# A fused transformer kernel: attention on 32-wide array tiles, split scales moved ahead, and a new order of loads, banks and ranks

## The chip, the cores and the metric

The kernel runs on one core of a Trainium2 chip. A core has a matrix engine (TensorE, PE in the rows; its loads of the stationary operand are listed apart as PEld), a vector engine (VectorE, DVE), an engine for activation functions (ScalarE, ACT), a general one (GpSimd, POOL), and SyncE (SP), which here only issues transfers. Each engine works through its own instructions in their order and waits at counting semaphores for the others. The metric is the device time of one launch, in microseconds; less is better.

## The reference

Four layers run one after the other on x of 2 batches x 1024 rows x 512 columns, each as `x = layernorm(x + layer(x))`:

```python
# 1: linear attention, 16 heads of 32
q, k, v = elu(x @ Wq.T) + 1, elu(x @ Wk.T) + 1, x @ Wv.T          # by head
kv = einsum('bhtd,bhte->bhde', k, v)
z  = 1 / (einsum('bhtd,bhd->bht', q, k.sum(axis=2)) + 1e-6)
y  = einsum('bhtd,bhde,bht->bhte', q, kv, z) @ Wo.T
# 2: feed-forward with packed fp4 weights, 1408 wide, a scale for each group of 128
w  = lut[nibble(packed)] * repeat(scales_f16, 128)
y  = rms_norm((silu(x @ w_gate.T) * (x @ w_up.T)) @ w_down.T)
# 3: gated linear attention (one head of 32 keys), gate, norm
q, k = softmax(x @ Wq.T), sigmoid(x @ Wk.T);  g = log_sigmoid(-k)
o  = gla_chunk(q, k, x, g)
go = o @ Wog.T + x @ Wig.T
y  = (rms_norm(o) * norm_w * silu(go)) @ Wo.T
# 4: a router picks the 512 best of each batch's 1024 rows; those pass an expert of 2048
s  = x @ router_w + router_b;  top, idx = top_k(s, 512)
y  = scatter_add(sigmoid(top) * (gelu(x[idx] @ w1 + b1) @ w2 + b2))
```

## The kernel before

All of it is written out by hand in two functions of engine blocks: for each engine a list of helper calls in the order in which they run, with semaphores between. Nothing else sets the order.

**Products.** A product of two float32 operands is made of three matmuls on rounded halves, `three_products` (L38): high x high (L41), high x low (L42), low x high (L43). ScalarE writes a high half, VectorE (or GpSimd) the low one by a subtraction. "A product" below means one such matmul of 512 columns.

**linear_attention (L150).** A batch b has 8 tiles of 128 rows, n or t. `tile_kv` projects a tile to keys and values (8 x 3 products), ScalarE takes exp and copies the values into v1 (with a column of ones, for the sum of the keys), `keys` on VectorE makes the feature map, and `add_kv` adds the tile's k^T v1 to an accumulator in PSUM. It takes a group g of four heads at once, so its 128x129 result also holds products of unlike heads. After the eighth tile `sums` masks these away (`kvz`). `query(b, h, m)` projects a half batch h of 512 rows to queries of the group m; `numerators(b, t)` multiplies a tile's queries by kvz (four matmuls of 128x132, one a group, the last four columns being the denominators); `attend` on VectorE divides; `transpose_att` turns the tile, `att_high` and `att_low` split it, and `project_out` multiplies by Wo; `finish` and `normalise` on VectorE end the layer norm. PSUM has eight banks of 512 columns. Beside all this VectorE and ScalarE unpack the fp4 weights of layer 2 (`nibbles`, `values`), and ScalarE widens the gate scales. A barrier of all engines ends the function.

**feed_forward_to_end (L843).** Layer 2 works on 4 blocks b of 512 rows and 11 tiles j of the hidden width, in units of half a tile (gate, then up). PE makes 4 groups a unit (L2127, L2128: two matmuls each), ScalarE scales the first group into an accumulator (L1257), VectorE adds the other three (`groups`, L1543, each with the group's scale), GpSimd multiplies gate by up and makes the low half, and PE runs the down product some tiles later. The down weights are made in block 0: for each tile j the row of fp16 scales is loaded to all partitions, VectorE splits it into a high and a low part (`down_scales(j)`, L1529 mask and L1532 subtraction, 128x512), and GpSimd multiplies the unpacked values by both (`down_weights`). Three of the eleven packed down tiles are unpacked here too, with one shift and one mask (`nibbles`, L1518 and L1520).

Layer 3 takes the same blocks as n = 0..3 (LAST = 3). In each, a loop over t makes scores and state of 128 rows (`update` L2213, `scores` L2220, `outputs`), then four gating steps (`silu`, `p_high`, `gated`, `p_low`) and the output projection with `y_bank(n, t)`, and `residual`, `variance`, `normalise` and `router` of the block before follow on VectorE while the next runs. Batch 0 is complete after block 1, so its ranks are counted while blocks 2 and 3 run: `rank(0, t)` compares a tile's scores with all (L1729), GpSimd `scatter`s row numbers and weights by rank, and `gather` fetches the 512 chosen rows, whose transposes (L2310) open layer 4. Meanwhile the expert's weights are loaded in chunks and split (`upper_half`, `lower_half`, L1704). Layer 4 runs `up(b, j)` and `down(b, j)` for batch 0, then 1, and `last_downs` ends it, tile by tile; `finish_selected(t)` (from L1787) makes the last rows.

## Time and profile before

| | |
|---|---|
| median of three runs | 1006.41 us (1006.1, 1006.41 and 1541.61) |
| profiled execution | 1005.34 us, span 1003.6 us |
| mean granted clock of PE | 0.986 of full speed |
| busy over the span | PE 928.8 us (93%), DVE 668.7 (67%), ACT 402.1 (40%), POOL 303.9 (30%) |
| moved | 52.64 MB, 52 GB/s |

The span runs from the first to the last instruction that the profiler shows; the time of the execution is 1.74 us longer. A busy share is an average over layers with different limits, and an engine may be busy and yet not be what the end waits for. The run of 1541.61 us stands far from the two others, and the median doesn't depend on it.

### The profile page before, as it was taken

To read this page: it belongs to the slowest core of one execution; us is meant where nothing else is said; L and a number is where in the kernel's file an instruction comes from. 1 tells how busy PE (TensorE), PEld (TensorE's weight loads), DVE (VectorE), ACT (ScalarE), POOL (GpSimd) and SP (SyncE) were. 2 spreads that over 40 slices of the span, in tenths; PEclk is the share of its full clock that TensorE was granted. 3 is DMA by queue.
4 is the path that set the end of the run, shared out by engine and by line. 5 is a ranking of instruction groups with operands and counts; after the bars stand their busy time and mean duration, and the time that the engine had idled before them with its cause. 6 is when DMAs were issued, how large, how long until landed. Compare 5 with 4: busy or idle time off the path is not lost.

```text
span 1003.6 us, 12375 instructions
## 1 busy us (share of the span) xinstructions
PE 928.8 (93%) x4182; PEld 728.5 (73%) x4182; DVE 668.7 (67%) x1325; ACT 402.1 (40%) x673; POOL 303.9 (30%) x270
## 2 busy tenths in 40 slices
PE   7998999898899999999998998999989989999993
PEld 5786788776576786776776666686857768878883
DVE  4666752666998778778856876866676777455413
ACT  4543022222334444454546367554454244323220
POOL 1000100001676543443333412232215322633333
PEclk9999999998999999999999999999999999999997
DMA  8433101201000000000010020010200444231411
GB/s 281 143 99 108 43 22 42 74 11 54 17 16 17 1 1 1 1 1 0 1 42 1 0 95 1 1 43 1 85 1 23 126 136 123 68 126 42 148 63 42
DMA packets 41792, 52.64 MB, mean 52 GB/s; under 512 B 5889, under 2 KB 23681, under 8 KB 41729
## 3 DMA queue, kind: packets, MB, share of 16 engines
q1 hardware_dynamic: 39904, 47.63, 14.7%
q0 software_dynamic: 1824, 4.22, 1.3%
q8 instruction: 34, 0.56, 0.2%
q14 instruction: 30, 0.24, 0.1%
HBM read 41.33 MB, written 10.50 MB: 52 GB/s over the span
## 4 chain that ended last, share of the span: by engine, by line
PE 42%; DVE 19%; issue 8%; ACT 4%; POOL 2%; DVEq 0%; ACTq 0%; POOLq 0%
PE ps_gla L41 10%; PE ps_gla L43 10%; PE ps_gla L42 10%; DVE acc L1543 9%; PE ps_gla L2127 4%; PE ps_gla L2128 4%; ACT acc L1257 1%; DVE junk L1729 1%; PE ps_gla L2227 1%; DVE router_junk L1697 1%; PE ps_gla L2157 1%; ACT fjunk L791 1%; PE ps_gla L2213 1%; DVE gsg L1655 1%; DVE scale_lo L1532 1%
## 5 line engine op out<-in xcount | busy, mean ns | idle before, releaser
L1543 DVE SCALAR_TENSOR_TENSOR acc<-ps_gla,gu_scale,acc 128x512 f32<-128x512 f32 x264 | 196.3, 749 | 64.9 <-ACT acc L1257 42.6
L2127 PE MATMUL ps_gla<-xt_hi,gu_val 128*128 128x512 f32 x352 | 147.3, 418 | 18.0 <-DVE acc L1543 7.0
L2128 PE MATMUL ps_gla<-xt_lo,gu_val 128*128 128x512 f32 x352 | 139.8, 397 | 0.0
L2127 PEld LDWEIGHTS ps_gla<-xt_hi,gu_val 128*128 128x128 f32 x352 | 67.2, 191 | 59.1 <-DVE acc L1543 40.7
L1257 ACT ACTIVATE acc<-ps_gla,gu_scale 128x512 f32<-128x512 f32 x88 | 60.5, 688 | 114.4 <-PE ps_gla L2128 114.4
L2034 POOL TENSOR_TENSOR fsg<-fsg,acc 128x512 f32<-128x512 f32 x44 | 62.1, 1412 | 129.3 <-DVE acc L1543 129.3
L616 POOL TENSOR_TENSOR a_rstd<-a_var,minus_half 128x1 f32<-128x1 f32 x16 | 10.8, 676 | 226.2 <-DVE a_var L508 226.2
L2128 PEld LDWEIGHTS ps_gla<-xt_lo,gu_val 128*128 128x128 f32 x352 | 67.5, 192 | 11.0
L2039 POOL TENSOR_TENSOR fh_lo<-fsg,fh_hi 128x512 fp32r<-128x512 f32 x44 | 56.8, 1291 | 51.8 <-ACT fh_hi L1269 51.8
L41 PE MATMUL ps_gla<-dn_hi,fh_hi 128*128 128x512 f32 x176 | 69.5, 395 | 0.0
L42 PE MATMUL ps_gla<-dn_hi,fh_lo 128*128 128x512 f32 x176 | 69.0, 392 | 0.0
L43 PE MATMUL ps_gla<-dn_lo,fh_hi 128*128 128x512 f32 x176 | 68.7, 390 | 0.0
L2091 POOL TENSOR_TENSOR mh_lo<-mh,mh_hi 128x512 fp32r<-128x512 f32 x32 | 42.3, 1322 | 82.3 <-ACT mh_hi L1502 82.2
L1497 ACT ACTIVATE mh<-ps_gla,b_sb 128x512 f32<-128x512 f32 x32 | 22.0, 687 | 96.7 <-PE ps_gla L43 94.0
L41 PE MATMUL ps_attn<-a_w_hi,xt_hi 128*128 128x512 f32 x128 | 52.5, 410 | 7.3 <-DVE a_w_lo L527 6.7
L41 PE MATMUL ps_gla<-mxt_hi,mw_hi 128*128 128x512 f32 x128 | 51.0, 398 | 3.9 <-DVE mw_lo L1704 2.9
L42 PE MATMUL ps_attn<-a_w_hi,xt_lo 128*128 128x512 f32 x128 | 51.1, 399 | 0.0
L43 PE MATMUL ps_attn<-a_w_lo,xt_hi 128*128 128x512 f32 x128 | 51.1, 399 | 0.0
L42 PE MATMUL ps_gla<-mxt_hi,mw_lo 128*128 128x512 f32 x128 | 50.5, 395 | 0.0
L43 PE MATMUL ps_gla<-mxt_lo,mw_hi 128*128 128x512 f32 x128 | 50.5, 394 | 0.0
L41 PE MATMUL ps_gla<-mw_hi,mh_hi 128*128 128x512 f32 x128 | 49.9, 390 | 0.0
L42 PE MATMUL ps_gla<-mw_hi,mh_lo 128*128 128x512 f32 x128 | 49.8, 389 | 0.0
(274 smaller groups left out, 2202.1 us busy)
## 6 DMA issues: line engine op xcount, KB each, us to landing
mw_raw<-in_w SPq DMA_DIRECT2D x16, 512.0 KB, 3.6
a_nib<-in_gate_up_packed SPq DMA_DIRECT2D x88, 64.0 KB, 2.2
x<-x SPq DMA_DIRECT2D x16, 256.0 KB, 3.6
mw_raw<-x SPq DMA_DIRECT2D x8, 512.0 KB, 4.4
out<-mw_raw SPq DMA_DIRECT2D x8, 512.0 KB, 3.0
xt_raw<-in_xT SPq DMA_DIRECT2D x3, 1024.0 KB, 5.1
x<-in_x SPq DMA_DIRECT2D x3, 1024.0 KB, 5.8
a_nib<-in_down_packed SPq DMA_DIRECT2D x8, 256.0 KB, 3.1
```

The source lines that it names most:

```text
L41: pe.matmul(out, lh, rh, start=first, stop=False)
L42: pe.matmul(out, ll, rh, start=False, stop=False)
L43: return pe.matmul(out, lh, rl, start=False, stop=last)
L616: pool.tensor_tensor(rstd[i % 2][:, :], var[i % 2][:, :], const.minus_half[:, 0:1], ALU.pow).then_inc(s_rstd, 1)
L1257: act.activation(acc[part][u // 2 % 2][:, :], ps[:, FG, :], ACT.Copy, scale=gu_scale[:, part * IT + j, 0:1]).then_inc(s_g0, 1)
L1497: act.activation(h[j % 2][:, :], ps[:, H + j % 4, :], ACT.Gelu_apprx_tanh, bias=b1_sb[:, j:j + 1]).then_inc(m_g, 1)
L1543: dve.scalar_tensor_tensor(out=a[:, :], in0=ps[:, FG + c, :], scalar=gu_scale[:, part * IT + j, c:c + 1], in1=a[:, :], op0=ALU.mult, op1=A ...
L2034: pool.tensor_tensor(f_sg[k % 2][:, :], f_sg[k % 2][:, :], acc[1][k % 2][:, :], ALU.mult).then_inc(s_h, 1)
L2039: pool.tensor_tensor(f_lo[k % HS][:, :], f_sg[k % 2][:, :], f_hi[k % HS][:, :].bitcast(F32), ALU.subtract).then_inc(s_hl, 1)
L2091: pool.tensor_tensor(h_lo[j % HS][:, :], h[j % 2][:, :], h_hi[j % HS][:, :].bitcast(F32), ALU.subtract).then_inc(m_hl, 1)
L2127: pe.matmul(ps[:, FG + c, :], gu_val[:, o, c, :], xt_hi[b % 2][:, c, :], start=True, stop=False)
L2128: pe.matmul(ps[:, FG + c, :], gu_val[:, o, c, :], xt_lo[b % 2][:, c, :], start=False, stop=True).then_inc(s_gu, 1)
```

## The change

1. **Array tiles.** `add_kv` makes one matmul for each of the 16 heads instead of four for groups: 32 columns of keys as the stationary operand, 33 columns of v1, into a 32-partition strip of one bank. `kvz` is then a plain copy. `numerators(b, t)` does tiles t and t + 1 in one call, 16 matmuls each that contract over the 32 rows of one head; the four heads of a group go to four banks. `attend` does three VectorE operations instead of five.
2. **Order in the attention.** The queries of the second half are projected earlier (0 before the first numerators, 1 before the first transposes, 2 after them), with places of their own (`q_next`) and a table of banks. Transposes, projections and VectorE's list follow in a new order.
3. **First loads.** SyncE loads Wk, then the second x tile, then Wv; PE starts with seven matmuls of ones, then the keys of tiles 0 and 1, then their values. ScalarE widens the gate scales at tile 5, not 0.
4. **Down scales.** They are split in the attention, on 11 partitions at once, stored to a scratch tensor in DRAM, and loaded from there to all partitions as two halves, into four buffers. `down_scales` goes; the nibble steps of block 0 are spread over units 3 to 8.
5. **Banks and ranks.** Below LAST `y_bank` alternates between two banks; in block 2 two ranks remain (of three), in block 3 the others stand elsewhere, as do `variance`, `normalise(2)`, `router(2)`, `lower_half(3)` and `pair_weights(0)`.
6. **End.** `last_downs` is called by piece; the final semaphores are cleared without a barrier behind.

```diff
@@ add_kv, numerators, attend @@
                 for g in range(KC):
-                    ins = pe.matmul(ps[:, KV0 + g // 2, (g % 2) * (P + 1):(g % 2 + 1) * (P + 1)], k[n % 2][:, g * P:(g + 1) * P],
-                                    v1[n % 2][:, g, :], start=(n == 0 and g % 2 == 0), stop=(n == NT - 1), skip_group_check=True)
+                    for j in range(HG):
+                        h = HG * g + j
+                        ins = pe.matmul(ps[j * DH:(j + 1) * DH, KV, g * (DH + 1):(g + 1) * (DH + 1)], k[n % 2][:, h * DH:(h + 1) * DH],
+                                        v1[n % 2][:, h, :], start=(n == 0 and g == 0), stop=(n == NT - 1), skip_group_check=True)
...
-                for g in range(KC):
-                    ins = pe.matmul(ps[:, PROJ + 2 * (t % 2) + g // 2, (g % 2) * (P + HG):(g % 2 + 1) * (P + HG)],
-                                    q[:, g, col:col + P], kvz[:, g, :], start=True, stop=True)
-                ins.then_inc(s_num, 1)
+                for u in (t, t + 1):
+                    for g in range(KC):
+                        for j in range(HG):
+                            d = slice(j * DH, (j + 1) * DH)
+                            ins = pe.matmul(ps[:, PROJ + j, num_col(u, g)], query_out(b, h, g)[d, (u % TB) * P:(u % TB + 1) * P], kvz[d, g, :],
+                                            start=True, stop=True)
+                    ins.then_inc(s_num, 1)
...
+                if i == 0:
+                    dve.wait_ge(s_dss, 32)
+                done(dve.tensor_scalar(z[:, :].rearrange("p (j g) -> p j g", j=HG), num[:, :, :, DH], 1e-6, None, ALU.add))
                 done(dve.reciprocal(zi[t % 2][:, :], z[:, :]))
...
@@ PE's list in the attention @@
+            warm_up(WARM)
             for b in range(NB):
-                tile_kv(b, 0)
-                if b:
-                    transpose_att(0, NT - 1)
+                if b == 0:
+                    for w in (WK, WV):
+                        tile_kv(b, 0, (w,))
+                        tile_kv(b, 1, (w,))
+                    add_kv(b, 0)
+                else:
+                    tile_kv(b, 0)
...
                     query(b, 0, m)
+                query(b, 1, 0)
                 numerators(b, 0)
-                numerators(b, 1)
+                query(b, 1, 1)
                 transpose_att(b, 0)
+                transpose_att(b, 1)
+                query(b, 1, 2)
                 numerators(b, 2)
...
@@ down scales: split in the attention, loaded as parts @@
+                        elif n == 6:
+                            dve.wait_ge(s_ds, 16)
+                            dve.tensor_scalar(dn_scale_hi[:, :].bitcast(U16), dn_scale16[:, :].bitcast(U16), 0xFFFE, None,
+                                              ALU.bitwise_and).then_inc(s_dsp, 1)
+                            dve.wait_ge(s_dsp, 1)
+                            dve.tensor_tensor(dn_scale_lo[:, :], dn_scale16[:, :], dn_scale_hi[:, :], ALU.subtract).then_inc(s_dsp, 1)
...
-                sp.dma_start(scale[j % 2][:, :], dn_scales[j:j + 1, :].to_broadcast([P, C])).then_inc(s_scl[j % 2], 16)
+                i = j % SCALES
+                if j >= SCALES:
+                    sp.wait_ge(s_dl, j - SCALES + 1)
+                sp.dma_start(scale_hi[i][:, :], dn_parts[0, j:j + 1, :].to_broadcast([P, C])).then_inc(s_scl[i], 16)
+                sp.dma_start(scale_lo[i][:, :], dn_parts[1, j:j + 1, :].to_broadcast([P, C])).then_inc(s_scl[i], 16)
...
@@ VectorE, gated attention @@
-                    if n == LAST:
-                        rank(0, 3 + t)
                     if n:
                         residual(n - 1, t)
                     if t:
                         o_low(n, t - 1)
-                if 0 < n < LAST:
+                    if n == LAST:
+                        rank(0, 2 + t)
+                if n:
                     variance(n - 1)
                 o_low(n, TB - 1)
                 mean_square(n)
+                if n == LAST:
+                    rank(0, 6)
+                    rank(0, 7)
...
                 if n == 2:
-                    for t in range(3):
+                    for t in range(2):
                         rank(0, t)
...
             variance(LAST)
+            lower_half(3)
             normalise(LAST)
             router(LAST)
...
@@ y_bank, and PE's end @@
-            return (Y, F)[t % 2] if n == LAST else Y
+            return (Y, F if n == LAST else G + 1)[t % 2]
...
-            for j in range(2, FT):
+            for j in range(2, FT - 1):
                 up(1, j)
                 down(1, j - 2)
-            last_downs(FT - 2)
+            up(1, FT - 1)
+            for t in range(2):
+                last_downs(t, range(FT - 3, FT - 1))
+            for t in range(2):
+                last_downs(t, range(FT - 1, FT))
+            for t in range(2, TB):
+                last_downs(t, range(FT - 3, FT))
```

How the instructions stand before, on PE, at the first numerators of batch 0 (a_q the queries, a_att a divided tile, a_at its transposed halves):

```order
L41 MATMUL ps_attn<-xt_hi_53,a_w_hi_63 128x512
L42 MATMUL ps_attn<-xt_hi_53,a_w_lo_67 128x512
L43 MATMUL ps_attn<-xt_lo_55,a_w_hi_63 128x512
L675 MATMUL ps_attn<-a_kvz,a_q 128x132 x8
L686 MATMUL ps_attn<-ident,a_att_74 128x128 x4
L675 MATMUL ps_attn<-a_kvz,a_q 128x132 x4
L686 MATMUL ps_attn<-ident,a_att_75 128x128 x4
L41 MATMUL ps_attn<-a_w_hi_64,a_at_hi_76 128x512
```

And now, at the same numerators:

```order
L41 MATMUL ps_attn<-xt_hi_54,a_w_hi_63 128x512
L42 MATMUL ps_attn<-xt_hi_54,a_w_lo_67 128x512
L43 MATMUL ps_attn<-xt_lo_56,a_w_hi_63 128x512
L740 MATMUL ps_attn<-a_kvz,a_q 128x33 x32
L41 MATMUL ps_attn<-xt_hi_54,a_w_hi_63 128x512
L42 MATMUL ps_attn<-xt_hi_54,a_w_lo_67 128x512
```

and where the first transposes follow:

```order
L41 MATMUL ps_attn<-xt_hi_54,a_w_hi_63 128x512
L42 MATMUL ps_attn<-xt_hi_54,a_w_lo_67 128x512
L43 MATMUL ps_attn<-xt_lo_56,a_w_hi_63 128x512
L753 MATMUL ps_attn<-ident,a_att_74 128x128 x4
L753 MATMUL ps_attn<-ident,a_att_75 128x128 x4
L41 MATMUL ps_attn<-xt_hi_54,a_w_hi_63 128x512
```

What moved: 32 tile matmuls stand at once for two tiles, with products of query(0,1,0) ahead of them; another projection of queries stands between them and the transposes, which now come in a pair.

VectorE in block 0 of the feed-forward, before (acc the accumulators of groups, scale_hi and scale_lo the split row, nib a packed tile):

```order
L1543 SCALAR_TENSOR_TENSOR acc_0_2649<-ps_gla,gu_scale,acc_0_2649 128x512 x3
L1529 TENSOR_SCALAR scale_hi_2664<-scale_2662 128x512
L1532 TENSOR_TENSOR scale_lo_2666<-scale_2662,scale_hi_2664 128x512
L1543 SCALAR_TENSOR_TENSOR acc_1_2648<-ps_gla,gu_scale,acc_1_2648 128x512 x3
L1543 SCALAR_TENSOR_TENSOR acc_1_2650<-ps_gla,gu_scale,acc_1_2650 128x512 x3
L1529 TENSOR_SCALAR scale_hi_2665<-scale_2663 128x512
L1532 TENSOR_TENSOR scale_lo_2667<-scale_2663,scale_hi_2665 128x512
L1518 TENSOR_SCALAR nib_2659<-nib_2659,shift 128x512
L1520 TENSOR_SCALAR nib_2659<-nib_2659 128x512
L1543 SCALAR_TENSOR_TENSOR acc_0_2647<-ps_gla,gu_scale,acc_0_2647 128x512 x3
```

and now:

```order
L1606 SCALAR_TENSOR_TENSOR acc_0_2997<-ps_gla,gu_scale,acc_0_2997 128x512 x3
L1606 SCALAR_TENSOR_TENSOR acc_0_2999<-ps_gla,gu_scale,acc_0_2999 128x512 x3
L1606 SCALAR_TENSOR_TENSOR acc_1_2998<-ps_gla,gu_scale,acc_1_2998 128x512 x3
L1606 SCALAR_TENSOR_TENSOR acc_1_3000<-ps_gla,gu_scale,acc_1_3000 128x512 x3
L1585 TENSOR_SCALAR nib_3009<-nib_3009,shift 128x512
L1606 SCALAR_TENSOR_TENSOR acc_0_2997<-ps_gla,gu_scale,acc_0_2997 128x512 x3
L1589 TENSOR_SCALAR nib_3009<-nib_3009 128x512
L1606 SCALAR_TENSOR_TENSOR acc_0_2999<-ps_gla,gu_scale,acc_0_2999 128x512 x3
L1585 TENSOR_SCALAR nib_3010<-nib_3010,shift 128x512
L1606 SCALAR_TENSOR_TENSOR acc_1_2998<-ps_gla,gu_scale,acc_1_2998 128x512 x3
```

What moved: the masks and subtractions of the scales are gone, and a nibble step stands alone between three accumulations and the next three.

VectorE in block 3 of the gated attention, after its last tile of outputs, before (junk and counts are a rank's, gsg the gate, x the rows):

```order
L1643 TENSOR_TENSOR o_lo<-ps_gla,o_hi 128x4x128 x2
L1649 TENSOR_SCALAR ms<-gss 128x4
L1655 TENSOR_TENSOR gsg_2707<-gsg_2707,o_f 128x512
L1655 TENSOR_TENSOR gsg_2708<-gsg_2708,o_f 128x512
L1729 TENSOR_SCALAR junk,counts<-scores_2749,score 128x896
L1729 TENSOR_SCALAR junk,counts<-scores_2749,score 128x128
L1734 SCALAR_TENSOR_TENSOR junk_own,counts<-scores_2749,score,before 128x128
L1738 SCALAR_TENSOR_TENSOR row<-counts 128x1
L1655 TENSOR_TENSOR gsg_2709<-gsg_2709,o_f 128x512
L1675 MEMSET gfiller 128x1
L1677 BN_AGGR gmv<-gst 128x2 x4
L1679 TENSOR_SCALAR gvar<-gmv 128x4
```

and now:

```order
L1706 TENSOR_TENSOR o_lo<-ps_gla,o_hi 128x4x128
L1712 TENSOR_SCALAR ms<-gss 128x4
L1792 TENSOR_SCALAR junk,counts<-scores_3101,score 128x768
L1792 TENSOR_SCALAR junk,counts<-scores_3101,score 128x256
L1797 SCALAR_TENSOR_TENSOR junk_own,counts<-scores_3101,score,before 128x128
L1801 SCALAR_TENSOR_TENSOR row<-counts 128x1
L1792 TENSOR_SCALAR junk,counts<-scores_3101,score 128x896
L1792 TENSOR_SCALAR junk,counts<-scores_3101,score 128x128
L1797 SCALAR_TENSOR_TENSOR junk_own,counts<-scores_3101,score,before 128x128
L1801 SCALAR_TENSOR_TENSOR row<-counts 128x1
L1718 TENSOR_TENSOR gsg_3059<-gsg_3059,o_f 128x512
L1747 TENSOR_SCALAR x_51<-x_51,gmv,grstd 128x512 x4
```

What moved: two ranks stand ahead of the first gating step, and block 2's normalisation behind it.

## Rows read from the trace of the kernel before

Columns of rows 1 and 10: stretch, its length, for PE, PEld, DVE, ACT and POOL the busy time and the number of instructions, PE's granted clock, share of the DMA engines, GB/s.

**Rows 1.** Busy time by stretch: attention, two feed-forward blocks, first block's start.

```profile
5.80:243.20 237.40, 219.31 (x1104) 183.35 (x1104) 145.12 (x341) 69.07 (x112) 10.82 (x16) 1.00 0.26 83
243.20:328.50 85.30, 76.88 (x300) 56.07 (x301) 74.42 (x97) 32.88 (x51) 50.81 (x42) 0.94 0.12 30
328.50:405.00 76.50, 74.98 (x326) 58.54 (x326) 60.92 (x94) 35.24 (x60) 34.46 (x26) 1.00 0.00 1
...
243.20:249.40 6.20, 6.14 (x15) 4.83 (x16) 2.96 (x5) 2.17 (x3) 0.42 (x2) 0.51 0.70 206
```

**Rows 2.** PE's waits in the attention: total, times, longest, in us.

```profile
PE ps_attn L675 <- DVE a_q L456: 4.0, 2, 2.0
PE ps_attn L686 <- DVE a_att L482: 3.7, 4, 1.4
PE ps_attn L41 <- DVE a_at_lo L493: 2.5, 2, 2.1
PE ps_attn L647 <- DVE a_k L448: 1.6, 1, 1.6
PE ps_attn L41 <- DVE xt_lo L429: 0.6, 1, 0.6
```

**Rows 3.** PE's waits from 735 to 830 us, same columns.

```profile
PE ps_gla L41 <- DVE mw_lo L1704: 2.9, 1, 2.9
PE ps_gla L2310 <- DMA xsel<-x,sel: 2.2, 1, 2.2
PE ps_gla L41 <- POOL p_lo L1961: 1.9, 1, 1.9
PE ps_gla L41 <- DVE x L1666: 1.4, 2, 0.9
```

**Rows 4.** Timeline of PE, 8 to 24 us: start, length, line, operands.

```profile
8.33 0.77 PE L41 MATMUL ps_attn<-a_w_hi,xt_hi 128*128 128x512 f32 x1 [0.89 <-DVE a_w_lo L527]
...
11.87 0.63 PE L43 MATMUL ps_attn<-a_w_lo,xt_hi 128*128 128x512 f32 x1
...
13.58 0.50 PE L41 MATMUL ps_attn<-a_w_hi,xt_hi 128*128 128x512 f32 x1
...
22.07 1.05 PE L647 MATMUL ps_attn<-a_v,a_k 128*128 128x129 f32 x8
...
23.19 0.40 PE L42 MATMUL ps_attn<-a_w_hi,xt_lo 128*128 128x512 f32 x1
23.42 0.39 PE L43 MATMUL ps_attn<-a_w_lo,xt_hi 128*128 128x512 f32 x1
```

**Rows 5.** Timeline of PE, 632 to 639 us, in the gated attention.

```profile
635.01 1.02 PE L2213 MATMUL ps_gla<-x,k_end 128*128 128x512 f32 x2
635.96 0.49 PE L2220 MATMUL ps_gla<-pair_t 64*128 64x128 f32 x2
...
636.71 0.39 PE L42 MATMUL ps_gla<-gw_hi,p_lo 128*128 128x512 f32 x1
```

**Rows 6.** Groups of PE by line, 590 to 1000 us: busy us, mean ns.

```profile
L2213 PE MATMUL ps_gla<-x,k_end 128*128 128x512 f32 x28 | 14.3, 594 | 0.0
```

**Rows 7.** Timeline of PE's weight loads, 625.8 to 630 us.

```profile
625.85 0.11 PEld L2204 LDWEIGHTS ps_gla<-ident,k_pair 128*64 128x64 f32 x1 [1.72 <-DVE k_end L1595]
625.88 0.11 PEld L2205 LDWEIGHTS ps_gla<-ident,q_pair 128*64 128x64 f32 x1
```

**Rows 8.** Groups of VectorE by line, 243 to 329 us: busy us, mean ns.

```profile
L1532 DVE TENSOR_TENSOR scale_lo<-scale,scale_hi 128x512 f16<-128x512 f16 x10 | 14.8, 1484 | 0.3
```

**Rows 9.** Waits from 243 to 329 us: total, times, longest.

```profile
PE ps_gla L2127 <- DVE acc L1543: 5.9, 4, 2.4
```

**Rows 10.** Busy time by stretch of 25 us, columns as in rows 1.

```profile
775.00:800.00 25.00, 22.85 (x103) 19.16 (x102) 17.19 (x41) 7.93 (x14) 9.59 (x8) 0.93 0.42 126
800.00:825.00 25.00, 22.09 (x87) 17.11 (x86) 18.92 (x34) 9.38 (x13) 5.78 (x4) 0.93 0.30 96
```

**Rows 11.** Timeline of VectorE, 982 to 1004 us.

```profile
984.23 0.75 DVE L1787 SCALAR_TENSOR_TENSOR xsel<-ps_gla,sel,xsel 128x512 f32<-128x512 f32 x1 [26.01 <-PE ps_gla L43]
...
990.56 0.75 DVE L1787 SCALAR_TENSOR_TENSOR xsel<-ps_gla,sel,xsel 128x512 f32<-128x512 f32 x1
```

373 lines of the change are left out of this document (200 added, 173 removed).

## The prediction

> **What bounds the kernel now.** I read the busy time by stage first. TensorE (PE) is the bound everywhere: it is busy for 219.31 of 237.40 us in the attention and for 74.98 of 76.50 in the second block of the feed-forward [rows 1]. So the change can gain in two ways only: by shorter work on PE, or by taking away PE's idle stretches and those at its lower clock. One stage stands out: the first block of the feed-forward takes 85.30 us with 300 matmuls, 0.284 us each, where the second takes 76.50 with 326, 0.235 each [rows 1]. At the second's pace the first would take 70.4, so 14.9 us are lost in it. The list of PE's waits, read for the attention and for the end of the gated attention, gives the rest [rows 2, 3]. The paces come from the timelines: a product of 512 columns costs 0.43 us at the start (clock at 1.2 GHz; four take from 11.87 to 13.58) and 0.23 later (2.4 GHz; 23.19 to 23.42) [rows 4].
>
> **Array tiles.** The change swaps 16 calls of add_kv, each of 4 matmuls of 128x129, for 16 matmuls of 33 columns, and 16 numerators of 4 matmuls of 128x132 for 8 double calls with 32 matmuls of 33 columns. Each f32 matmul is two passes: the row of add_kv says x8 for 4 calls [rows 4]. So 256 passes become 1024. Before, the 8 passes and the first product behind them take from 22.07 to 23.19, 1.12 us, of which the product is 0.23: 0.89 a call, 0.112 a pass [rows 4]; 256 passes are 28.6 us. No 32-row or 32-column tile is in the trace. The nearest is L2220, which contracts over 64 rows. From the start of L2213 (two passes of 0.43: 1.02 together less the 0.59 of one in flight [rows 5, 6]) to the second product behind L2220 are 1.70 us (635.01 to 636.71). At the paces of full-size work it would be 0.86 + 2 x 0.112 + 0.23 = 1.31. The detour to smaller tiles costs 0.39 us [rows 5]. Weight loads are evidently not hidden across it. With 16 + 8 = 24 detours that is 24 x 0.39 = +9.4 us. The passes themselves I bound from both sides. If nothing overlaps and each keeps the 0.112, they cost 1024 x 0.112 = 114.7, or +86. If all four tiles run at once, a pass costs a quarter, 0.028, and the sum is 28.7, or 0. Lower still: in add_kv the loads too have only 32 of 128 columns, so 512 of the passes could cost a quarter again, 0.007 each, a gain of 10.7. I take 0: the four tiles of a group have separate rows or columns and nothing in the order makes one wait for another, and the least distance between two weight loads in the trace, 0.03 us (625.85 and 625.88), allows it [rows 7]. Tiles: **+9.4** (-1.3 to +95).
>
> By the Trainium skill, "TensorE: Matmul & The Clock Gate", section "Wait - 56ns, not 53.3ns?", a matmul can cost about 62 ns of the sequencer, which binds when the array's work is shorter. That speaks against this change: 1024 x 0.062 is 63.5 us, 34.9 over the 28.6 now, and the sum below would come to 1017. The bursts of the trace have at most 16 passes of 0.112 and do not show which holds.
>
> **Order in the attention.** PE waits 4.0 us for the query features before the numerators, 3.7 for the attended rows before their transposes and 2.5 for the low halves before the output projection: 10.2 in both batches [rows 2]. The new order puts a whole projection (12 products of 0.23, 2.7 us) before each of these points: query(1,0) ahead of the first numerators, query(1,1) ahead of the first transposes, query(1,2) ahead of the first output projection. The longest of these waits is 2.1, less than 2.7. What is late next is VectorE in the second half of a batch: queries(1,3), x_low(2), two attends, then att_low(4) and att_low(5) with finish(2) and finish(3) between them. I leave 3.6 of the 10.2 there and take **-6.6** (-2 to -9). The scales' split adds two VectorE operations on 11 partitions and two stores; attend(0,0) now waits for these stores, with numerators and transposes queued on PE behind it, but query(1,1) covers it; if the stores land late (they follow a 1 MB load on SP's queue), it costs a microsecond, which stands in the bounds. At add_kv(1) PE waits 1.6 for keys [rows 2], because ScalarE stands before the second key's exponential for the gate scales' load; that conversion moves to the sixth tile: **-1.6**.
>
> **First loads.** Two waits follow the first product: 0.89 for the next weights and 0.6 for the other tiles' low half [rows 2, 4]. Now K is projected for two tiles, while V's weights arrive, so both waits can go (-1.5). Seven warm-up matmuls of ones run while PE would stand idle, so they cost nothing themselves. If they bring the 2.4 GHz level forward, products of 0.43 become 0.23; from 8.33 to 13.58 twelve run at the low level, 0.20 too much each, 2.4 us [rows 4]. The weights' low halves come chunk by chunk from VectorE, which the 0.89 shows to be barely ahead, so not all of it is to be had: -1.5. Sum **-3** (0 to -4).
>
> **First block of the feed-forward.** Out of VectorE go 11 masks and 11 subtractions, of which scale_lo takes 1.48 each [rows 8]; the six nibble steps stay, but one a unit instead of two back to back. PE's recorded waits for accumulation are 5.9 there [rows 9], and short ones and the half-speed stretches after them make up the rest of the 14.9. Of that some 3.4 is the start after the barrier between the phases, which stays: the clock of the first 6.20 us is 0.51, which alone is 3.0 us of work [rows 1]. Of the 11.5 left, three come back where a nibble step still meets six accumulations: **-8.5** (-5 to -11). GpSimd now waits for the loads of the parts instead of for VectorE, with f_low and so PE's down products behind it; four buffers and a load that is issued three tiles ahead cover that, and if not, one load shows, once.
>
> **Ranks, banks, routing.** A rank stands before the last gating of block 2 and delays the p_lo for which PE waits 1.9; one of the three goes. In block 3 the residual comes ahead of the rank, and the second bank takes the rest of the 1.4 that the projection waits [rows 3]: -3 of 3.3. Ranks 6 and 7 now come before the gatings, in a gap in which VectorE waits for PE anyway, so that the pairs are scattered some 5 us earlier, and the gather no longer holds PE for 2.2. The low half of chunk 3 moves ahead of normalise and router, and 2.9 goes [rows 3]. After each of these two the clock falls: 0.93 over 25 us is 1.75 us lost, and it does so in two stretches one behind the other, 3.5 [rows 10]. Together 8.6; what is next is the diagonals' product, 1.2 us later for the moved subtraction: **-7.5**. Ranks, banks and routing: **-10.5** (-5 to -13).
>
> **End.** VectorE finishes the four last tiles in one run from 984.23 to the start of the last at 990.56, a tile every 2.1 us [rows 11]. PE's work is the same, but the first two tiles are whole earlier, and the barrier after the semaphores are cleared is gone: **-1.5** (0 to -2).
>
> **Sum.** +9.4 - 6.6 - 1.6 - 3 - 8.5 - 10.5 - 1.5 = -22.3 on a profiled execution of 1005.34, whose span is 1003.6. That gives 983.0. The three runs' median of 1006.41 is 1.07 above it; halved between them, I forecast **983.5**.
>
> **Rivals.**
> Tiles better than a quarter: 32-column loads at once bring the 10.7 of the lower bound, 983.5 - 10.7 = **973**. For it: nothing in the trace forbids it. Against: no row shows a start under 0.03 [rows 7].
> The waits return: with PE's gaps closed VectorE becomes the bound in attention and routing, and half of the 31.7 us of gains is lost: **999**. For it: VectorE has 145 of 237 us in the attention, in bursts [rows 1]. Against: what is left of work between the waits grows by nothing.
> Starts bind: if load and matmul each take the 0.03 of [rows 7], a pass costs 0.06, 1024 make 61.4, +32.8: **1016**.
> Slower: weight loads of tiles do not overlap and every pass keeps 0.112: +86, **1070**, in add_kv and the numerators. From 0.070 us a pass (28.6 and the 43 between 983.5 and 1026.5, over 1024) it is over 2% slower than now. For it: at L2220 the detour shows loads laid bare. Against: those two loads share their rows.
> That the split scales merely move their time is part of the second rival: two operations of 11 partitions can't carry 19 us.
>
> **Chances.** Forecast 0.42; better tiles 0.18; waits return 0.20; starts bind 0.12; serial 0.08. The range goes from 965 to 1007: it takes in the first three cases and leaves out the last two, 0.2. A measurement of this kernel tells about 2% from no change, that is below 986.3. Faster by more: most of the first, all of the second, 0.55; slower by more 0.08; within 0.37.
>
> **What would show it.** In the trace of the changed kernel: the starts around the 16-fold matmuls of add_kv (1.3 us from the first to the next product: right; 0.9: better; over 2: starts bind); the first block near 77 us; no wait for xsel and mw_lo, and clock 1.00 there; attention waits of some 4 us. The forecast is wrong if the tiles' passes cost far from 0.028, since that term is multiplied by 1024.

## The result, and the profile after

The changed kernel takes 961.5 us (median of four runs, 961.3 to 963.81); the kernel before took 1006.88 beside it (median of four runs, one of them the run of 1541.61 us; the three others have 1006.41). The ratio is 0.9557, with a 95% interval of 0.9537 to 0.9577. The forecast was 983.5 and the range ended at 965: the time lies below it. The profiled execution has a span of 959.3 us against 1003.6, 44.3 less.

The head of the page, its row of PE and its chain of work:

```profile
span 959.3 us, 13818 instructions
...
PE 918.3 (96%) x4964; PEld 719.2 (75%) x4964; DVE 648.4 (68%) x1268; ACT 400.2 (42%) x674; POOL 302.2 (32%) x270
...
PE 58%; DVE 10%; issue 3%; ACT 3%; POOL 1%; DVEq 0%; ACTq 0%; POOLq 0%
```

The busy time by stretch, the same program stages as in [rows 1] (attention, block 0, block 1, and the first 6.2 us of block 0):

```profile
5.80:228.60 222.80, 213.66 (x1872) 172.26 (x1872) 141.93 (x306) 68.61 (x113) 10.57 (x16) 0.99 0.28 89
228.60:301.70 73.10, 71.88 (x300) 55.87 (x301) 55.78 (x76) 32.10 (x51) 49.31 (x42) 0.96 0.20 55
301.70:377.80 76.10, 74.70 (x325) 58.65 (x325) 59.45 (x92) 35.13 (x60) 34.27 (x26) 1.00 0.00 1
...
228.60:234.80 6.20, 6.12 (x16) 4.90 (x17) 2.95 (x5) 2.14 (x3) 0.41 (x2) 0.57 0.66 189
```

The attention is 14.6 us shorter, though PE issues 1872 passes in it where it issued 1104. Block 0 of the feed-forward fell from 85.30 to 73.10 us, with the same 300 matmuls; its start still runs at about half the clock (0.57).

PE's waits in the attention (total, times, longest):

```profile
PE ps_attn L41 <- DVE a_w_lo L557: 2.5, 2, 1.5
PE ps_attn L753 <- DVE a_att L515: 1.4, 2, 0.9
PE ps_attn L41 <- issue: 0.6, 2, 0.3
PE ps_attn L41 <- DVE a_q L498: 0.4, 1, 0.4
PE ps_attn L740 <- issue: 0.4, 1, 0.4
```

Of the 10.2 us of waits for a_q, a_att and a_at_lo in [rows 2], 1.8 are left; the one for a_k is gone, and so are in block 0 those for VectorE's accumulators, the 5.9 of [rows 9]: this is what is left of them between 229 and 302 us, beside the barrier.

```profile
PE ps_gla L2192 <- PEq L71: 4.7, 1, 4.7
PE ps_gla L2222 <- DVE acc L1606: 0.4, 2, 0.2
```

And from 675 to 830 us, which takes in the stretch of [rows 3], one wait of PE is left:

```profile
PE ps_gla L2285 <- ACT pair_t L1370: 1.3, 1, 1.3
```

To say where the 44.3 us went I read, in the timelines of PE, when each execution reaches the same points of the program:

| PE reaches | before | changed | gained since the row above |
|---|---|---|---|
| the last add_kv of batch 0 | 65.68 | 60.02 | 5.7 |
| the first add_kv of batch 1 | 136.76 | 127.78 | 3.3 |
| the last add_kv of batch 1 | 178.47 | 167.48 | 2.0 |
| the feed-forward's block 0 | 243.26 | 228.68 | 3.6 |
| block 1 | 328.55 | 301.76 | 12.2 |
| block 0 of the gated attention | 581.18 | 553.94 | 0.5 |
| its block 2 | 681.83 | 652.64 | 1.9 |
| its block 3 | 735.80 | 706.61 | 0.0 |
| the transposes of the first chosen rows | 795.57 | 759.29 | 7.1 |
| those of batch 1 | 895.31 | 852.82 | 6.2 |
| the end of the span | 1003.62 | 959.30 | 1.8 |

Each column is one execution, and the first rows move from one to the next. In the eleven profiled runs of this document whose PE list up to the barrier is the changed kernel's (gate_scales_back, no_warm, warm_more, warm_fewer and the kernels in strip order left out), the last add_kv of batch 0 stands between 58.7 and 60.9 us, the first of batch 1 between 127.8 and 130.0, and the feed-forward's block 0, where its start is the changed kernel's too, between 228.7 and 231.8. The column above has the earliest of the last two, so the 14.6 us of the attention are the upper end of what it gained. Block 0 takes 72.3 to 73.1 us in the executions that leave it as it is, and from block 0 of the gated attention on the stretches that an edit leaves alone agree to 0.4 us.

### The profile page after: what moved, and what is told of

Same layout as the page of the kernel before. It is cut to its first block, busy times and chain, and to the rows that moved or that the text cites. A ratio compares the mean times of both kernels' runs of the same rounds, so it can differ in the third digit from the quotient of the medians.

```text
span 959.3 us, 13818 instructions
## 1 busy us (share of the span) xinstructions
PE 918.3 (96%) x4964; PEld 719.2 (75%) x4964; DVE 648.4 (68%) x1268; ACT 400.2 (42%) x674; POOL 302.2 (32%) x270
## 4 chain that ended last, share of the span: by engine, by line
PE 58%; DVE 10%; issue 3%; ACT 3%; POOL 1%; DVEq 0%; ACTq 0%; POOLq 0%
PE ps_gla L41 14%; PE ps_gla L43 13%; PE ps_gla L42 13%; DVE acc L1606 6%; PE ps_gla L2192 6%; PE ps_gla L2193 5%; PE ps_gla L2292 1%; ACT acc L1324 1%; PE ps_gla L2278 1%; ACT fjunk L864 1%; PE ps_gla L2222 1%; PE ps_gla L2304 1%; PE ps_gla L2285 1%; DVE x L878 0%; POOL mh_lo L2156 0%
## 5 line engine op out<-in xcount | busy, mean ns | idle before, releaser
L2192 PE MATMUL ps_gla<-xt_hi,gu_val 128*128 128x512 f32 x352 | 145.2, 412 | 11.1 <-PEq L71 4.7
L43 PE MATMUL ps_gla<-mw_lo,mh_hi 128*128 128x512 f32 x128 | 49.8, 389 | 0.0
```

The source lines that it names most:

```text
L43: return pe.matmul(out, lh, rl, start=False, stop=last)
L2192: pe.matmul(ps[:, FG + c, :], gu_val[:, o, c, :], xt_hi[b % 2][:, c, :], start=True, stop=False)
```

## The tiles

The timeline of PE around an add_kv and around a double call of numerators:

```profile
20.01 0.39 PE L43 MATMUL ps_attn<-a_w_lo,xt_hi 128*128 128x512 f32 x1
20.32 0.46 PE L699 MATMUL ps_attn<-a_v,a_k 128*32 128x33 f32 x32
20.71 0.50 PE L41 MATMUL ps_attn<-a_w_hi,xt_hi 128*128 128x512 f32 x1
21.05 0.39 PE L42 MATMUL ps_attn<-a_w_hi,xt_lo 128*128 128x512 f32 x1
```

```profile
71.86 0.39 PE L43 MATMUL ps_attn<-xt_lo,a_w_hi 128*128 128x512 f32 x1
72.35 1.99 PE L740 MATMUL ps_attn<-a_kvz,a_q 32*128 32x33 f32 x64
74.27 0.50 PE L41 MATMUL ps_attn<-xt_hi,a_w_hi 128*128 128x512 f32 x1
74.61 0.39 PE L42 MATMUL ps_attn<-xt_hi,a_w_lo 128*128 128x512 f32 x1
```

The 32 passes of add_kv start within 0.39 us, up to the next product. From the product ahead to the second one behind, 20.01 to 21.05, it is 1.04 us where it was 1.35 (21.84 to 23.19). Less the two products in it, a call costs 0.59 us and cost 0.89 (as worked out from [rows 4]): 16 calls gain 4.9. The detour is really there (0.32 us of a call: PE starts the first tile 0.09 later than a product would, and the products behind it later by 0.12 and 0.11). The 32 passes themselves take 0.27 us, 0.0085 each, a third of the 0.028 that I took and near the lower bound of 0.007. The 64 passes of the numerators take 1.8 us, 0.028 each, as forecast (0.027 from start to start). Where products stand on both sides a double call costs 2.12 us, less these products, and two calls cost 1.8 before: 8 times, 2.5 us lost (the first call, shown above, has 0.2 us more ahead of it). Together the tiles gain 2.4 us; the forecast had them lose 9.4.

Why they are this fast was tested by the order in which the heads are taken. In the changed kernel neighbours stand in different strips of 32 columns (add_kv) or rows (numerators).

**kv_strip_order**

```diff
-                for g in range(KC):
-                    for j in range(HG):
+                for j in range(HG):
+                    for g in range(KC):
                         h = HG * g + j
```

> The changed kernel (961.5 us), but add_kv goes through the heads strip by strip: the four matmuls of one 32-column strip stand one behind the other, where they alternated between the four strips. In the changed kernel a pass of add_kv starts every 0.0085 us. Theory 1, the strips work side by side and only neighbours in other strips overlap: a pass costs four times as much, 0.034, so 32 x 0.0255 = 0.82 us a call, 16 calls, +13 us, 974.5. Theory 2, a pass is short because only 33 columns move and 32 are loaded, whatever strip it is in: no change, 960 to 963.

964.81 us (964.57 to 967.36). The timeline of PE:

```profile
19.65 0.90 PE L699 MATMUL ps_attn<-a_v,a_k 128*32 128x33 f32 x32
20.48 0.50 PE L41 MATMUL ps_attn<-a_w_hi,xt_hi 128*128 128x512 f32 x1
20.82 0.39 PE L42 MATMUL ps_attn<-a_w_hi,xt_lo 128*128 128x512 f32 x1
```

The burst takes 0.83 us to the next product instead of 0.39, 0.44 more: a pass costs 0.023. So theory 1 is right that neighbours in other strips overlap, and wrong in the size: within one strip a pass of 33 columns costs 0.023, not 0.034. Sixteen calls are 7.1 us more on PE. The time rose by 3.3: 2.2 come back between the last add_kv of batch 0 and the first of batch 1 (65.6 us here, 67.8 in the changed kernel), where PE had waited for VectorE's queries and attended rows, and this execution's first add_kv stands 0.7 earlier.

**num_strip_order**

```diff
-                    for g in range(KC):
-                        for j in range(HG):
+                    for j in range(HG):
+                        for g in range(KC):
                             d = slice(j * DH, (j + 1) * DH)
```

> The changed kernel, but the numerators go through a tile row strip by row strip: four matmuls on the same 32 rows one behind the other, where they alternated between the four strips. A pass there takes 0.028 us (64 in 1.8 us), a quarter of the 0.112 of before. Theory 1, side by side: a pass costs 0.112 again, 64 x 0.084 = 5.4 us a call, 8 calls, +43 us, 1004. Theory 2, the pass's own size (33 columns move): no change, 960 to 963. Between: only the weight loads overlap across strips, some +10 to +25.

1000.04 us (998.79 to 1000.92), near theory 1. The timeline of PE, and the busy time by stretch with the granted clock in its third number from the end:

```profile
72.55 4.36 PE L740 MATMUL ps_attn<-a_kvz,a_q 32*128 32x33 f32 x64 [0.55 <-DVE a_q L498]
76.83 0.73 PE L41 MATMUL ps_attn<-xt_hi,a_w_hi 128*128 128x512 f32 x1
77.36 0.63 PE L42 MATMUL ps_attn<-xt_hi,a_w_lo 128*128 128x512 f32 x1
77.79 0.63 PE L43 MATMUL ps_attn<-xt_lo,a_w_hi 128*128 128x512 f32 x1
```

```profile
72.00:76.80 4.80, 4.25 (x64) 4.28 (x64) 2.34 (x5) 1.75 (x3) 0.00 (x0) 1.00 0.90 268
76.80:80.00 3.20, 3.20 (x9) 2.49 (x9) 2.14 (x6) 0.00 (x0) 0.00 (x0) 0.52 1.02 353
```

The same 64 passes take 4.28 us instead of 1.92: 0.067 each, and not the 0.112 of theory 1, whose 1004 us is met for another reason in part. In the single records neighbours in one strip stand 0.11 us apart, the price of a pass of full size, though only 33 columns move; the next strip's passes run beside them at the turns. Eight calls at 2.4 us more, at least, are 19 us. The other half of the 38 is the clock: behind the first burst products take 0.43 us, and the clock of that stretch is 0.52, with no idle time in between. A stretch at 0.50 or 0.51 begins at most 1.3 us behind each of the first four bursts (at 76.9, 90.6, 107.7 and 117.9 us) and inside each of the last four (at 196.4, 210.1, 230.6 and 244.2), 44 us in all, where the changed kernel has a clock of 1.00 from 60 us to its last attention product. The last four bursts run partly in such stretches and are slower still, 4.8 to 6.2 us, so the two halves can't be told apart to the microsecond.

So the order of the heads decides the worth of this change: strip by strip in the numerators would have left 7.9 us of the gain of 45 (the kernel before took 1007.96 beside it).

## Block 0 of the feed-forward

**masks_back**

```diff
                     if b == 0:
+                        dve.tensor_scalar(dummy[1][:, :].bitcast(U16), dummy[0][:, :].bitcast(U16), 0xFFFE, None,
+                                          ALU.bitwise_and).then_inc(s_dummy, 1)
+                        dve.wait_ge(s_dummy, 2 * j + 2)
+                        dve.tensor_tensor(dummy[1][:, :], dummy[0][:, :], dummy[1][:, :], ALU.subtract).then_inc(s_dummy, 1)
                         nibble_step(2 * j + 1)
```

> The changed kernel with the same two operations (mask and subtraction, 128x512 fp16) put back on VectorE behind each second unit of block 0, on a buffer of their own that nobody waits for; the rest stays. Block 0 takes 73.1 us now and took 85.3. Theory 1, VectorE's time was the loss: 11 x 1.77 = 19.5 us more work against PE's slack in each tile of about 1 us, block 0 comes to 79 to 84, the time to 968 to 972. Theory 2, the loss was the run of nibble steps or GpSimd's wait for the split parts: block 0 stays under 75, 961 to 963.

972.43 us (971.05 to 973.62), theory 1, at the top of its range. Block 0, and PE's wait in it:

```profile
229.90:311.50 81.60, 75.26 (x301) 54.05 (x302) 71.90 (x98) 33.17 (x51) 50.60 (x42) 0.98 0.17 49
```

```profile
PE ps_gla L2200 <- DVE acc L1608: 3.6, 4, 1.2
```

It takes 81.6 us, 8.5 more than in the changed kernel's profile, for 19.4 us of operations.

**nibbles_paired**

```diff
                 if u in (3, 5, 7):
                     shift_nibbles((u - 3) // 2)
-                elif u in (4, 6, 8):
-                    mask_nibbles((u - 4) // 2)
+                    mask_nibbles((u - 3) // 2)
```

> The changed kernel, but shift and mask of a packed tile stand back to back again behind one unit (2.6 us together, three times). Theory 1, VectorE has enough slack in block 0 once the scales' operations are gone: 961 to 963. Theory 2, a step a unit is what hides them: each pair shows 1 to 1.5 us on PE and the half-speed clock behind it, +3 to +6, 965 to 967.

962.8 us (959.94 to 963.69), theory 1: block 0 takes 73.8 us, 0.7 to 1.5 more than in the executions that have the changed kernel's block 0. The pairs were not what was expected, though: shift and mask take 0.48 and 1.40 us there, 1.9 together, and not the 2.6 of the kernel before (1.38 and 1.26).

**masks_nibbles_back** has masks_back's edit and this one, and no step behind the first units:

```diff
                     if b == 0:
                         ...
-                        nibble_step(2 * j + 1)
+                        if 1 <= j < 1 + IT - DN_SLOTS:
+                            shift_nibbles(j - 1)
+                            mask_nibbles(j - 1)
```

> As masks_back (block 0 took 81.6 us there), and shift and mask of a packed tile again back to back right behind the scales' two operations, behind the second units of tiles 1 to 3. If the order of VectorE's work is the rest of the loss, block 0 comes to 84 to 85.5 (85.3 before), 975 to 976.5. If the rest was GpSimd's wait for VectorE's halves, which this kernel does not have, it stays at 81 to 82, 972.

975.58 us (974.52 to 977.25). Block 0, and PE's wait in it:

```profile
228.80:314.20 85.40, 77.11 (x301) 56.10 (x301) 74.79 (x98) 33.05 (x51) 51.20 (x42) 0.94 0.17 47
```

```profile
PE ps_gla L2200 <- DVE acc L1608: 5.8, 4, 2.4
```

85.40 us: block 0 of the kernel before to 0.1 us, and its waits with it, 5.8 us for 5.9. The whole gain of 12.2 is VectorE's: 8.5 for the scales' operations, 3.8 more for the nibble steps in a run with them, and nearly nothing for the steps' order alone. GpSimd's wait for VectorE's halves, which these kernels do not have, plays no part.

The 3.8 are not only a matter of the run. A shift or mask of the same 128x512 elements takes 0.42 to 0.48 us in some places and 1.25 to 1.42 in others. In the five traces each of the 21 long ones has operations of GpSimd beside it for at least three quarters of its time, and the 9 short ones start while GpSimd is idle. masks_back has the three masks in such gaps (0.42 each), masks_nibbles_back has them beside GpSimd (1.26 each): 2.5 us more work on VectorE by their place alone. In the kernel before the six steps took 7.9 us, in the changed kernel 5.7. So the steps' place gained in two ways, and no run here separates them.

## The start of the attention

**no_warm**

```diff
-        WARM = 7
+        WARM = 0
```

> The changed kernel without the seven matmuls of ones ahead of the first product. Theory 1, as predicted: they bring 2.4 GHz forward; without them the products up to 13.5 us run at 0.43 instead of 0.23, and the time is 1.5 to 2.4 us longer, 963 to 964. Theory 2: the first products wait for the weights' low halves and, later, for VectorE's queries at 64 us (idle 0.4 now, 2.2 in a run whose start went faster), so what the start loses comes back there: 961 to 962.

961.51 us (960.8 to 962.3): the matmuls of ones are worth nothing that can be measured, theory 2 in size. Its first products, and those of the changed kernel:

```profile
5.91 0.76 PE L41 MATMUL ps_attn<-a_w_hi,xt_hi 128*128 128x512 f32 x1 [5.91 <-DVE a_w_lo L557]
...
7.89 0.77 PE L41 MATMUL ps_attn<-a_w_hi,xt_hi 128*128 128x512 f32 x1 [0.36 <-DVE a_w_lo L557]
...
9.73 0.51 PE L42 MATMUL ps_attn<-a_w_hi,xt_lo 128*128 128x512 f32 x1
10.09 0.40 PE L43 MATMUL ps_attn<-a_w_lo,xt_hi 128*128 128x512 f32 x1
10.32 0.40 PE L41 MATMUL ps_attn<-a_w_hi,xt_hi 128*128 128x512 f32 x1
```

```profile
6.21 0.40 PE L42 MATMUL ps_attn<-a_w_hi,xt_lo 128*128 128x512 f32 x1
6.45 0.39 PE L43 MATMUL ps_attn<-a_w_lo,xt_hi 128*128 128x512 f32 x1
8.34 0.47 PE L41 MATMUL ps_attn<-a_w_hi,xt_hi 128*128 128x512 f32 x1 [1.50 <-DVE a_w_lo L557]
...
9.02 0.63 PE L43 MATMUL ps_attn<-a_w_lo,xt_hi 128*128 128x512 f32 x1
9.45 0.63 PE L41 MATMUL ps_attn<-a_w_hi,xt_hi 128*128 128x512 f32 x1
```

With them the first product runs at 2.4 GHz (6.21 to 6.45 is 0.24), then PE idles 1.5 us for the second chunk, and from 9.02 on products take 0.43 again. Without them the products of 0.43 come earlier. Nor do the ones bring the higher clock each time: in the changed kernel's run **control** below, with the same seven, products take 0.43 from the first on, to 13.7 us. The first add_kv stands at 19.28 us without them and at 20.32 with them; in the runs here whose start is the changed kernel's own it stands between 19.0 and 21.2, so nothing of the ones can be seen in it.

**gate_scales_back**

```diff
                         if n == 0:
                             x_high(1)
+                            act.wait_ge(s_gs, 16)
+                            act.activation(gu_scale[:, :, :], gu_scale16[:, :, :], ACT.Copy).then_inc(s_gsc, 1)
...
-                        elif n == 5:
-                            act.wait_ge(s_gs, 16)
-                            act.activation(gu_scale[:, :, :], gu_scale16[:, :, :], ACT.Copy).then_inc(s_gsc, 1)
```

> The changed kernel with ScalarE's widening of the gate scales at the first tile of the attention again, where it waits for their load. Predicted was 1.6 us for this move, from PE's wait for keys at 30 us. Theory 1: the wait comes back and shows, +1.6, 963. Theory 2: it comes back, and PE's wait for the queries at 64 us (0.4 to 2.3 in these runs) shrinks by as much: 961 to 962.

969.28 us (968.84 to 969.75): 7.8 more, and neither theory. The second add_kv:

```profile
31.53 0.67 PE L698 MATMUL ps_attn<-a_v,a_k 128*32 128x33 f32 x32 [6.36 <-DVE a_k L486]
32.13 0.80 PE L41 MATMUL ps_attn<-a_w_hi,xt_hi 128*128 128x512 f32 x1
```

PE waits 6.4 us here, and runs at half speed behind it. In the kernel before it waited 1.6 for keys that stood behind the same transfer, and started this call at 30.22. The new first loads bring PE to the call at 25.2 us instead of 28.6, and the transfer lands later, not earlier: SyncE issues it at 24.57 us, where it was 23.22, and ScalarE starts to widen the scales at 29.53, where it was 28.21. So with ScalarE standing before the scales the first loads would have gained nothing, and the two edits have to be priced together. Together they gain 3.5 us up to the last add_kv of batch 0 (5.7 less the 2.1 of seven tiled calls), and between 2.7 and 4.8 by the spread of that point.

## The gated attention, the routing and the end

**decays_back**

```diff
-                if n < LAST:
-                    decays(n + 1)
                 p_high(n, 1)
                 if n == 0:
                     fold_norm_w(range(2, KC))
+                if n < LAST:
+                    decays(n + 1)
```

> The changed kernel with ScalarE's decays(n + 1) again behind p_high(n, 1) in blocks 0 to 2 of the gated attention. The prediction gave this move no term; block 1 to 2 took 55.2 us before and 53.1 now, and the waits for k_end (1.30) and pair_t (1.52) at 626 to 629 us are gone. Theory 1, this move took them away: +2 to +3, 963.5 to 964.5, and these waits come back at 599 us. Theory 2, the second bank or the ranks did: no wait comes back, 961 to 962.

964.3 us (964.25 to 964.55), theory 1. The waits come back where they were expected:

```profile
599.59 0.30 PE L2269 MATMUL ps_gla<-ident,k_pair 128*64 128x128 f32 x1 [1.29 <-DVE k_end L1658]
...
602.92 0.37 PE L2285 MATMUL ps_gla<-pair_t 64*128 64x128 f32 x1 [1.52 <-ACT pair_t L1370]
```

From block 0 to block 2 of the gated attention it takes 100.6 us again, as before (100.65), and 98.7 in the changed kernel: 1.9 of the 2.8.

**ranks_back**

```diff
+                    if n == LAST:
+                        rank(0, 3 + t)
                     if n:
                         residual(n - 1, t)
                     if t:
                         o_low(n, t - 1)
-                    if n == LAST:
-                        rank(0, 2 + t)
...
-                if n == LAST:
-                    rank(0, 6)
-                    rank(0, 7)
...
                 else:
+                    rank(0, 7)
                     router(2)
...
-                    for t in range(2):
+                    for t in range(3):
```

and GpSimd's scatters accordingly.

> The changed kernel with three ranks in block 2 and ranks 3 to 6 ahead of the residuals of block 3, rank 7 ahead of router(2), and the scatters where they stood, as before; banks, variance, normalise, router and the low halves stay as changed. Theory 1, the ranks' places caused the waits for p_lo (1.9), for x (1.4) and for the gathered rows (2.2), and the fall of the clock behind the last: +5 to +8, 967 to 969. Theory 2, the second bank and the earlier normalise had taken most of it: +0 to +2.

967.07 us (963.82 to 969.01), theory 1, at its lower end by the median. PE's waits from 705 to 830 us:

```profile
PE ps_gla L2371 <- DMA xsel<-x,sel: 1.4, 1, 1.4
...
PE ps_gla L2301 <- DVE o_lo L1706: 0.9, 1, 0.9
PE ps_gla L41 <- POOL p_lo L2025: 0.7, 1, 0.7
```

From block 3 to the transposes it takes 56.3 us, against 52.7 in the changed kernel and 59.8 before. So the ranks' places are 3.6 of the 7.1 us gained there. In its profiled execution the feed-forward begins 2.2 us later (230.87 against 228.68), which the edit doesn't touch, so the ranks account for less than the 5.6 us of the medians. The other half of the 7.1 stays with the edits that this kernel keeps, among them the places of variance, normalise and router of block 2; that it is these was not shown.

**lower3_back**

```diff
             variance(LAST)
-            lower_half(3)
             normalise(LAST)
             router(LAST)
             diagonals(1)
-            for n in range(4, 6):
+            for n in range(3, 6):
                 lower_half(n)
```

> The changed kernel with the low half of chunk 3 again behind normalise, router and diagonals of the last block, as before. Theory 1, this place alone made PE wait 2.9 us for mw_lo and run at half speed for 3.4 us behind it (1.7 lost): +4 to +5, 966. Theory 2, since all of VectorE's list is less late now: under +1.

965.75 us (964.52 to 968.88), theory 1. The wait is there again:

```profile
PE ps_gla L41 <- DVE mw_lo L1767: 2.9, 1, 2.9
```

From the first transposes to the second it takes 98.1 us, against 93.5 in the changed kernel and 99.7 before: 4.5 for one wait of 2.9 and the half-speed stretch behind it.

**one_bank**

```diff
-            return (Y, F if n == LAST else G + 1)[t % 2]
+            return (Y, F)[t % 2] if n == LAST else Y
...
-                pe.wait_ge(s_r, max(i - 1, TB * n))
+                pe.wait_ge(s_r, max(i - 1, TB * n) if n == LAST else i)
```

> The changed kernel with one bank for the output projection of blocks 0 to 2 of the gated attention, as before, so that each tile's projection waits for the residual of the one before. Theory 1: a residual (0.7 us on VectorE, 1 us with its start) lies on the path at 12 tiles' turns, +3 to +9. Theory 2: transposes and states of the next block stand between the projections and hide it: +0 to +1, as the trace of before showed 2 waits for x of 1.4 together.

960.38 us (959.44 to 961.47), theory 2: the second bank is worth nothing, with everything else as it now stands.

**last_downs_back**

```diff
-            for j in range(2, FT - 1):
+            for j in range(2, FT):
                 up(1, j)
                 down(1, j - 2)
...
+            for t in range(TB):
+                last_downs(t, range(FT - 2, FT))
```

> The changed kernel with the last products in their old order, two hidden tiles for each of the four row tiles in turn. Predicted: the new order is worth 0 to 1 us at the end: 961.5 to 962.5. PE's own work is the same. From PE's last product to the end of the span were 15.4 us before and are 13.1 now: if the order made this difference, +2.3.

962.58 us (961.5 to 965.21), as expected. From the start of PE's last matmul to the end it takes 14.2 us, against 13.5 in the changed kernel and 15.7 before. But the last matmul itself comes later by the new order, so a fixed point has to be taken: from the transposes of batch 1 to the end it takes 106.7 us, against 106.5 and 108.3. The order of the last products is worth 0.2 to 0.3 of the 1.8, the rest belongs to the other edits at the end.

## A faster version

Two more idle stretches of PE stand in the changed kernel's trace: 1.5 us after the first chunk's products, and 4.7 at the barrier, each with a half-speed stretch behind it. **warm_at_barrier** fills the second:

```diff
             project_out(1, NT - 2)
             project_out(1, NT - 1)
+            warm_up(18)
```

> The changed kernel with 18 matmuls of ones (4 us) on PE behind the last output projection of the attention, ahead of the barrier, where PE waits 4.7 us. Theory 1: the half-speed start of the feed-forward is owed to this idle time; with PE busy until the barrier the first 6 us run at 2.4 GHz and 2.5 to 3 us go: 958.5 to 959.5. Theory 2: the barrier comes later by the matmuls, or the idle rest of the barrier suffices to lower the clock: 961.5 to 963.

962.2 us (960.47 to 962.71), no gain. Block 0 took 71.6 us, 0.7 to 1.5 less than in the changed kernel's executions, but it started 5.2 us behind the last product's end, not 4.7: 18 are too many. **warm_more** adds this to it:

```diff
                         ins = three_products(pe, ps[:, bank + w, :], xt_hi[h][:, c, t * P:(t + 1) * P], xt_lo[h][:, c, t * P:(t + 1) * P],
                                              w_hi[w][:, c, :], w_lo[w][:, c, :], c == 0, c == KC - 1)
+                        if i == 0 and w == WK and c == 0:
+                            warm_up(6)
```

> As warm_at_barrier, and six more matmuls of ones (1.3 us) between the first chunk's products and the second's, where PE waits 1.5 us for the weights' low half. If the clock's fall at 9 us (0.43 a product up to 12.0) comes from that wait, products stay at 0.23: the start gains 1.4 us, of which what VectorE's queries at 64 us leave shows: 0.3 to 1.4 below warm_at_barrier, 957.5 to 959. If the matmuls of ones delay the second chunk instead, up to 1 us above it.

961.09 us (959.53 to 963.84), not clear of the changed kernel. **warm_fewer** is the same with `warm_up(14)` ahead of the barrier.

> As warm_more, but 14 matmuls of ones ahead of the barrier instead of 18, since 18 ended 1.2 us ahead of the feed-forward's start, which came 5.2 us behind the last product instead of 4.7. With 14 (3.2 us) the start should stand at 4.7 again and still be at 2.4 GHz: 0.5 below warm_more, 1.5 to 2.5 below the changed kernel, 959 to 960. If the clock falls in the 1.5 us that are left idle, block 0 takes 73 us again, 961.5.

959.58 us (958.39 to 961.68). It was run again in five rounds, beside the changed kernel itself:

> The changed kernel itself once more, on the same chip and in the same rounds as the next one: 961 to 962.5.

> warm_fewer again in five rounds, beside the changed kernel. In its trace block 0 took 71.5 us against 73.1, at 2.4 GHz from its first product: -1.5 there, and up to -1 from the start of the attention: 959 to 960, 1.5 to 2.5 below the control. If the 1.9 us of the first measurement were chance, it equals the control.

The changed kernel took 961.4 us (961.14 to 964.38), this one 959.46 (959.22 to 960.61): 1.9 less, and none of its runs reaches the other's fastest. The start of block 0 in its trace:

```profile
PE ps_gla L2196 <- PEq L71: 1.5, 1, 1.5
```

```profile
226.00:232.00 6.00, 4.32 (x16) 2.85 (x17) 3.05 (x6) 2.68 (x4) 0.42 (x2) 1.00 0.42 128
```

PE is idle for 1.5 us at most there, and the clock stays at 1.00, where it was 0.57 at the changed kernel's start of block 0. Which of the two places earns the 1.9 us is not shown. In the two traces of this pair of runs block 0 is only 0.75 us shorter (71.5 against 72.3), while the first add_kv stands at 18.85 us against 21.18, with products of 0.23 us from the first on; and that point moves by 2 us between executions that start alike. The ones at the barrier alone gained nothing, with 18 of them.

## Why the prediction was wrong

By its own steps (the last column is read from the changed kernel's profiled execution; the order in the attention is what is left of the attention's 14.6 us after the tiles and the first loads):

| step | forecast | measured |
|---|---|---|
| array tiles | +9.4 | -2.4 |
| order in the attention | -6.6 | -8.7 |
| gate scales and first loads | -1.6 - 3 | -3.5 |
| block 0 | -8.5 | -12.2 |
| blocks 1 to 3 | 0 | -0.5 |
| ranks, banks, routing | -10.5 | -15.2 |
| end | -1.5 | -1.8 |
| sum | -22.3 | -44.3 |

1. **The tiles' passes.** The step that failed is "I take 0", the pass at a quarter of 0.112 in all calls; with the detour it makes 11.8 of the 22.0 us by which the sum is off. In the numerators it held (0.028). In add_kv it was 0.0085, which is 10 us over 512 passes. The text had it as the lower bound and as the first rival, and named the reason: there the loads too have only 32 of 128 columns. I set it aside because no row showed a start under 0.03 us, an argument from two loads of 64 columns, which are not such a load. The detour of 0.39 was nearly right (0.32, another 1.7 us over 24). The rule of the Trainium skill that the prediction weighed ("TensorE: Matmul & The Clock Gate", section "Wait - 56ns, not 53.3ns?") has a condition that the prediction left out: it gives some 62 ns of the sequencer for a matmul with hardware decode off. It does not bind here: 32 passes are started in 0.39 us.
2. **Block 0.** "Three come back where a nibble step still meets six accumulations" did not happen: alone, the steps cost some 1 us even in pairs. An operation on VectorE costs there what PE's slack does not take up: 19.4 us of masks and subtractions cost 8.5, and with the nibble steps in one run they cost 12.3. The loss that stays was put at 3.4, and is 2.7 (73.1 less the 70.4 of the second block's pace).
3. **Ranks, banks, routing.** In block 3 and the routing 11.6 us of waits and slow stretches were told one by one, and 13.3 went; the 1.2 us that "is next" by the moved subtraction did not show. The other 1.9 have no term in the prediction: ScalarE's decays stood in the change as a line among others, and the waits that they caused (1.30 and 1.52 us at 626 to 629 us) lay outside the stretches whose waits the prediction used. One reason was wrong: the second bank, which was to take part of 3 us, is worth nothing in the run that takes it out; the size came from elsewhere, which is luck.
4. **Order in the attention.** "I leave 3.6 of the 10.2" was too much, 1.8 of waits are left. The waits went where a projection of 2.7 us was put ahead of them, as the prediction had it; no run puts the old order back, so this rests on the waits alone.
5. **First loads.** Size nearly right, price of the parts wrong: the matmuls of ones gave nothing, and the gate scales' move, put at 1.6, holds 7.8 in the new order. The wait for the next weights, which was to go, is 1.5 us in the changed kernel (0.89 before). That the sum of the two terms fits is luck.
6. The rival of the waits that return did not come, nor the two of dear starts; the run in strip order shows that a dearer pass exists (0.067), in an order that the change does not use. Of the prediction's signs the first block (near 77 us) and the attention's waits (some 4 us) came out lower, at 73.1 and 1.8.

The forecast of 983.5 and the first rival of 973 erred to the same side by the points 2 to 4, which are 10.5 us together: better tiles alone would have left the time inside the range.

## What to carry to other kernels

Small matmuls on separate strips of the array are worth having when neighbours in program order stand in different strips: the same work cost 961.5 us in one order of heads and 1000.0 in the other. Where an engine that paces another has extra work in one block, price it by what the other's slack leaves over and not by its sum (here 19.4 us of operations cost 8.5, and the nibble steps some 1 alone but 3.8 on top of them), and look whether its operations take longer beside another engine's. An edit that lets PE arrive earlier at a wait is worth nothing alone, and the wait's own edit looks small alone; price such pairs together, and read the waits of the whole program, not only around the edits that look big.

## What the runs showed of the hardware

- Passes of 128x33 on four column strips in turn start 0.0085 us apart (32 in 0.27 us), in one strip 0.023; passes that contract over 32 rows, with a stationary operand of 128 columns, 0.028 in turn and 0.067 in the order strip by strip, with single distances of 0.11. From a product to tiles and back costs 0.32 us.
- The clock fell to 0.52 directly behind a burst of 4.3 us of passes on one strip after the other, in which PE was not idle. Behind bursts on four strips in turn of 1.9 us products went on at 0.23 us.
- Shifts and masks of 128x512 int32 on VectorE took 0.42 to 0.48 us when they started while GpSimd was idle, and 1.25 to 1.42 beside an operation of GpSimd.
- Idle stretches of 1.5 us at 6.8 us and of 4.7 at the barrier were followed by products of 0.43; matmuls of ones that left 1.5 us idle at the barrier kept the products at 0.23. So 1.5 us of idle time came before a fall in one place and not in the other.
